# The first of 32 chunks of a recommendation kernel is loaded, multiplied and contracted in two halves, the second among layer 2's first banks, and ScalarE issues 11 of the first half's 23 loads

## What is computed

```python
e = jnp.stack([tbl_0[ids[:, 0]], ..., tbl_38[ids[:, 38]]], axis=1)      # (1024, 39, 16)
def _cin_layer(x0, xk, W, b):
    out = jnp.einsum('bhd,bmd,shm->bsd', xk, x0, W) + b[None, :, None]
    return jax.nn.relu(out)
x1 = _cin_layer(e, e, W1, b1)        # W1 (128, 39, 39)
x2 = _cin_layer(e, x1, W2, b2)       # W2 (128, 128, 39)
z = concatenate([x1.sum(-1), x2.sum(-1)], -1)
h = relu(concatenate([z, dense_ctx], 1) @ W_top1 + b_top1)
y = relu(h @ W_top2 + b_top2) @ W_top3
```

## Time and profile before

| | |
|---|---|
| median of 3 runs | 1172.12 us (1167.8 to 1173.06) |
| the profiled execution, its own time | 1171.53 us |
| its span, first to last instruction | 1169.7 us |
| PE busy, share of the span | 1089.3 us, 93% |
| DVE busy | 981.9 us, 84% |
| ACT busy | 822.2 us, 70% |
| POOL busy | 850.0 us, 73% |
| mean granted clock of TensorE | 0.999 |

### The profile page before, as it was taken

One profiled execution on the slowest core, in us unless ns is written; L12 is line 12 of the kernel. 1 busy time (PEld: TensorE's weight loads), 2 busy tenths in 40 slices (PEclk: granted clock), 3 DMA queues, 4 the chain that ended last, 5 costly groups with the idle time before them and its releaser, 6 DMA issues.

```text
span 1169.7 us, 18115 instructions
## 1 busy us (share of the span) xinstructions
PE 1089.3 (93%) x4475; PEld 824.1 (70%) x4475; DVE 981.9 (84%) x2893; ACT 822.2 (70%) x2774; POOL 850.0 (73%) x951
## 2 busy tenths in 40 slices
PE   0069999999999999999999999999999999999998
PEld 0037677677777777767777667777777777777687
DVE  4048999998988989998998668998899989996787
ACT  5027677777777777777777667777777777775774
POOL 7756888878787888788878758787887864543454
PEclk9999999999999999999999999999999999999999
DMA  6178678685877678684876538776787858665342
GB/s 182 29 161 182 123 145 179 147 168 106 188 163 147 135 154 180 145 168 100 195 162 150 110 70 189 167 145 130 154 185 154 168 110 201 146 147 104 73 85 52
DMA packets 82881, 166.61 MB, mean 142 GB/s; under 512 B 17812, under 2 KB 31014, under 8 KB 82775
## 3 DMA queue, kind: packets, MB, share of 16 engines
q0 software_dynamic: 28272, 85.81, 42.2%
q1 hardware_dynamic: 54502, 79.64, 24.3%
HBM read 78.36 MB, written 3.81 MB: 70 GB/s over the span
## 4 chain that ended last, share of the span: by engine, by line
PE 83%; DVE 9%; POOL 3%; issue 2%; SPq 1%; ACT 1%; DMA 1%; DVEq 0%; ACTq 0%
PE bank L821 66%; PE l_acc L806 14%; DVE acc L680 4%; POOL emb L404 3%; DVE t_sum L688 1%; PE misc L854 1%; PE misc L850 1%; DVE p2acc L698 1%; DVE x1l L645 0%; DVE p L721 0%; SPq L359 0%; DVE t_sum L692 0%; ACT prod L527 0%; DVE p1acc L655 0%; SPq L366 0%
## 5 line engine op out<-in xcount | busy, mean ns | idle before, releaser
L527 ACT ACTIVATE prod<-bank,emb 128x128 f32<-128x128 f32 x2552 | 715.8, 380 | 272.0 <-PE bank L821 269.5
L680 DVE SCALAR_TENSOR_TENSOR acc<-bank,emb,acc 128x128 f32<-128x128 f32 x2184 | 612.5, 345 | 68.1 <-PE bank L821 67.3
L821 PE MATMUL bank<-w2h,x1h 128*128 128x512 f32 (+1 forms) x1280 | 537.0, 420 | 10.4 <-DVE acc L680 8.2
L821 PE MATMUL bank<-w2l,x1h 128*128 128x512 f32 (+1 forms) x1280 | 494.4, 386 | 0.0
L821 PE MATMUL bank<-w2h,x1l 128*128 128x512 f32 (+1 forms) x1280 | 449.7, 417 | 0.0
L404 POOL DMA_INDIRECT emb<-tbl,idx x312 | 312.5, 1001 | 82.5 <-issue 77.9
L821 PEld LDWEIGHTS bank<-w2h,x1h 128*128 128x128 f32 x1280 | 241.0, 188 | 106.3 <-issue 44.7
L821 PEld LDWEIGHTS bank<-w2h,x1l 128*128 128x128 f32 x1280 | 240.6, 188 | 74.2 <-issue 20.3
L821 PEld LDWEIGHTS bank<-w2l,x1h 128*128 128x128 f32 x1280 | 241.0, 188 | 61.1 <-issue 22.1
L424 POOL TENSOR_TENSOR tree<-prod 128x640 f32<-128x640 f32 x127 | 237.2, 1868 | 55.0 <-DMA prod<-prod 55.0
L415 POOL DMA_DIRECT2D prod<-prod x127 | 123.6, 973 | 170.2 <-ACT prod L527 170.1
(11 more groups left out here) (105 smaller groups left out, 421.4 us busy)
## 6 DMA issues: line engine op xcount, KB each, us to landing
prod<-prod POOLq DMA_DIRECT2D x127, 640.0 KB
z<-e_rows SPq DMA_DIRECT2D x96, 234.0 KB
z<-e_rows SPq DMA_DIRECT2D x192, 78.0 KB
z<-e_rows SPq DMA_DIRECT2D x96, 156.0 KB
emb<-tbl,idx POOLq DMA_INDIRECT x312, 4.9
prod<-w_by_h SPq DMA_DIRECT2D x3, 832.0 KB, 8.4
z<-e_rows SPq DMA_DIRECT2D x32, 66.0 KB
e_rows<-e_t SPq DMA_DIRECT2D x8, 256.0 KB
```

Of the source, the lines that this page charges most:

```text
L527: last = nc.scalar.activation(prod[:, ct % P_RING, i, n * S:(n + 1) * S], bank[:, (ct * NB + k) % RING, n * S:(n + 1) * S], ACT.Copy, scal ...
L680: nc.vector.scalar_tensor_tensor(dst, src, scale, dst if step else b2_row[:, :], ALU.mult, ALU.add).then_inc(v_step, 1)
L821: last = nc.tensor.matmul(out_bank[:, 0:b - a], x, w[:, a:b], start=(n == 0), stop=(n == 2))
```

## The change

Chunk 0 is split into two halves of 256 columns. Half 0 runs ahead of the loop as the chunk did before. Half 1 is worked in among chunk 0's own banks: DVE makes its products at g = 1, 2, 3, PE contracts it at g = 7, 8, 9 and 11 into the PSUM tile `misc`, ACT ends it at g = 12, DVE forms `x1l` at g = 13; position 2 (g = 20) is the first that needs it. Half 1 multiplies from the SBUF rows without a copy to `e_rep`. Chunk 1's steps move: `copy_rep(1)` from ahead of bank 0 to between banks 0 and 2 on ACT, its seven products to g = 4, 6, 8, 11, 14, 16, 19 with `REST` fifth instead of third, its first contractions to g = 13, 15 and on. The loads of half 0 are shared: SP issues 12 (replicated rows, groups 1 and 2), ACT the other 11 (group 3, both factors of `REST`). SP issues all 23 of half 1 and then chunk 1's. Every transfer of a half moves the same number of rows as before, each of 1 KB instead of 2 KB.

```diff
+MAKE_SECOND_AT = (4, 6, 8, 11, 14, 16, 19)
+HALF = CH // 2
+HALF_MAKE_AT = {1: (0, 1, 2), 2: (3, 4), 3: (5, 6)}
+HALF_CONTRACT_AT = {7: (0, 1), 8: (2, 3), 9: (4, 5), 11: (6,)}
+HALF_ROUND_AT, HALF_MIX_AT = 5, 6
+HALF_X1_AT, HALF_X1L_AT, HALF_P1_AT = 12, 13, 14
...
-    if f == 0:
-        return tuple(range(NF))
+    if f == 1:
+        return (0, 1, 2, 3, REST, 4, 5)
...
+    if f == 1:
+        return {13: 0, 15: 1, 17: 2, 20: 3, 23: REST, 24: 4, 25: 5}
...
-                load_shifted(f)
                 if f == 0:
-                    load_rest_first(0)
+                    sp.wait_ge(et_stored[0], 64)
+                    load_half_rep(sp, 0)
+                    load_half_group(sp, 0, 0)
+                    load_half_group(sp, 0, 1)
+                    load_half_rep(sp, 1)
+                    for k in range(len(Z_GROUPS)):
+                        load_half_group(sp, 1, k)
+                    load_half_first(sp, 1)
+                    load_half_second(sp, 1)
+                else:
+                    load_shifted(f)
...
-            copy_rep(0)
-            for c in range(-1, CHUNKS):
+            act.wait_ge(et_stored[0], 64)
+            load_half_group(act, 0, 2)
+            load_half_first(act, 0)
+            copy_rep_half()
+            load_half_second(act, 0)
+            round_rest_half(0)
+            end_layer1_half(0)
+            for c in range(CHUNKS):
                 f = c + 1
                 for g in range(GB):
+                    if c == 0 and g == 1:
+                        copy_rep(1)
+                    if c == 0 and g == HALF_ROUND_AT:
+                        round_rest_half(1)
+                    if c == 0 and g == HALF_X1_AT:
+                        end_layer1_half(1)
...
+            def make_half(h, t):
+                rows = F_ROWS[t]
+                part = z[0:rows, 0, t, half(h)]
+                if t == REST:
+                    dve.wait_ge(half_first[h], 64)
+                    dve.wait_ge(half_second[h], 64)
+                    first = rest[0:rows, half(h)].bitcast(F32)
...
+                    first = z[0:rows, 0, NF, half(1)] if h else e_rep[0:rows, half(0)]
+                nc.vector.tensor_tensor(part, first, part, ALU.mult).then_inc(f_made if h else half_made, 1)
...
+                if c == 0 and j == 2 and k == 0:
+                    pe.wait_ge(x1l_done, 1)
```

More of the change, by code:

```diff
@@ L264, in gathers_before, with loads, half @@
             return min((TILES - 1) * M, -(-M * (ct + 9 + min(2, ct // 4)) // 16))
+        def loads(f):
+            return (f + 1) // 2
+        def half(h):
+            return slice(h * HALF, (h + 1) * HALF)
+        half_acc = (l1_acc[:, 0:HALF], misc[:, 0:HALF])
         def wait_early(eng, tile):
@@ L345, in load_shifted @@
                 wait(sp, f_used, NF * (f - 1))
-                wait(sp, rep_ready, f - 1)
+                wait(sp, rep_ready, f - 2)
                 def rows(first, ap):
@@ L510, in round_rest, with copy_rep_half, round_rest_half, end_layer1_half @@
                 nc.scalar.copy(rest[0:3 * N_REST, :], z[0:3 * N_REST, f % 2, REST, :]).then_inc(rest_high, 1)
+            def copy_rep_half():
+                act.wait_ge(half_rep[0], 64)
+                nc.scalar.copy(e_rep[:, half(0)], z[:, 0, NF, half(0)]).then_inc(half_copied, 1)
+            def round_rest_half(h):
+                part, parts = rest[0:3 * N_REST, half(h)], z[0:3 * N_REST, 0, REST, half(h)]
+                act.wait_ge(f_made if h else half_made, NF)
+                nc.scalar.copy(part, parts).then_inc(rest_high if h else half_high, 1)
+            def end_layer1_half(h):
+                act.wait_ge(f_used if h else half_used, NF)
+                nc.scalar.activation(half_acc[h], half_acc[h], ACT.Relu, bias=bias1[:, 0:1]
+                                     ).then_inc(x1_relu if h else half_relu, 1)
+                act.wait_ge(x1_relu if h else half_relu, 1)
+                nc.scalar.copy(x1h[:, 0, half(h)], half_acc[h]).then_inc(x1h_done if h else half_x1h, 1)
             def end_layer1(f):
@@ L747, in _ @@
                                         ).then_inc(top_split, 1)
-            for c in range(-1, CHUNKS):
+            for t in range(NF):
+                make_half(0, t)
+            mix_rest_half(0)
+            make_x1l_half(0)
+            sum_p1_half(0)
+            for c in range(CHUNKS):
                 f = c + 1
@@ L794, in contract @@
                 rows = F_ROWS[t]
-                if turn == 0:
-                    pe.wait_ge(w1_summed, 1)
-                    wait(pe, l1_free, f)
-                    wait(pe, x1l_done, f)
+                if turn == 0 and f == 1:
+                    pe.wait_ge(half_summed, 1)
+                    pe.wait_ge(half_x1l, 1)
+                if turn == 0 and f > 1:
+                    pe.wait_ge(l1_free, f)
+                    pe.wait_ge(x1l_done, f)
                 if t == REST:
@@ L806, in contract, with contract_half @@
                 nc.tensor.matmul(l1_acc[:, :], w, x, start=(turn == 0), stop=(turn == NF - 1)).then_inc(f_used, 1)
+            def contract_half(h, t):
+                rows = F_ROWS[t]
+                if t == 0:
+                    pe.wait_ge(w1_summed, 1)
+                if t == REST:
+                    pe.wait_ge(w_rest_mixed, 1)
+                    pe.wait_ge(rest_mixed if h else half_mixed, 1)
+                    w, x = w_rest[0:rows, :], rest[0:rows, half(h)]
+                else:
+                    pe.wait_ge(f_made if h else half_made, t + 1)
+                    w, x = w1[0:rows, t, :], z[0:rows, 0, t, half(h)]
+                nc.tensor.matmul(half_acc[h], w, x, start=(t == 0), stop=(t == REST)
+                                 ).then_inc(f_used if h else half_used, 1)
             def layer2_bank(c, j, k):
```

110 lines of the change are left out of this document (91 added, 19 removed).

## The result

The changed kernel takes 1177.76 us, the median of 11 runs (1173.45 to 1183.17); the kernel before, run beside it, takes 1168.66 (11 runs, 1164.4 to 1173.17). The ratio is 1.0068, 95% interval 1.0048 to 1.0088: slower by 5.6 to 10.3 us. The forecast was 2.4 us faster, 1169.7, with 1166 to 1174.5 as its range. It was wrong: the time moved the other way, by 9.1 us, and ended above the range, just under the 1178 beyond which the forecast had put 7 chances in 100. The profiled execution of the changed kernel took 1179.83 us, with a span of 1178.0.

A forecast was written before the change was run, and what follows sets the result against it. The prediction took PE, without slack from bank 0 on, as the bound, with loads and a chain of steps setting bank 0's start. Its terms, -6.6 + 2.7 + 1.5 = -2.4 us, gave 1169.7 us, range 1166 to 1174.5.

The forecast's parts named there:

- What bounds the kernel: PE is busy 99 to 100% from bank 0 on, so each us of earlier start or added wait counts at the end.
- Term 1: Before bank 0: half-width loads shared by SP and ACT start bank 0 at 71.4 instead of 77.96 us, -6.6 us.
- a packet of 1 KB lies between: Half 0's loads: 1 KB packets take 55 ns, so 1,078 of them move at 160 a us, in 6.7 us.
- is issued at 64.2: ACT's 11 loads of half 0: 7.3 us of issue and a 0.4 us copy, last one landing at 66.1.
- Term 2: Half 1's contractions on PE, formerly in idle time, now stand between chunk 0's banks: +2.7 us, called certain.
- Term 3: Chunk 0's banks: ACT waits for chunk 1's replicated rows, PE stalls before bank 7, +1.1 us; DVE's readout adds +0.4.
- due 3.4 us later than before: Chunk 1's last load meets product `REST` at g = 14 with five banks of slack behind it, at no cost.
- A PE wait among banks 15 to 20, released by DVE: Sign that the forecast is wrong: chunk 1's `REST` loads would come past 91.5 us.
- Small packets are no cheaper: Rival, 12 in 100: loads stay at 96 packets a us, bank 0 at 75.5, total 1175.2 us, or 1178.5 with backlog.
- ACT's issues are dear: Case inside the forecast: 1 us per ACT issue, bank 0 at 73.2, term 3's first part gone, -2.1 us in all.
- No wait at copy_rep(1): Rival, 18 in 100: chunk 1's replicated rows land by 76.5, term 3 is 0 to 0.2, total 1168.2 to 1166.4 us.
- Merges fall differently: Rival, 8 in 100: the 31 merges on DVE, at another phase to GpSimd, give or take 3 us or so.

The follow-up runs named there:

- e6: The changed kernel again, unchanged, beside the kernel before on another chip: 1177.09 us, ratio 1.0057 to the kernel before.
- e12: The kernel before, with GpSimd holding back tile 1's gathers until the first chunk's loads have landed: 1172.44 us in one run.
- e13: The changed kernel, with SP alone issuing all 23 loads of half 0: 1183.1 us, ratio 1.0101 to the kernel before.
- e11: The changed kernel, with SP issuing nothing of half 1 before all of half 0 has landed: 1180.37 us in one run.
- e9: The kernel before, with ScalarE issuing 11 of the first chunk's 23 loads, all in full width: 1171.59 us, ratio 1.0022.
- e8: The kernel before, with each of the first chunk's 23 loads cut into two pieces of 256 columns, all issued by SP: 1186.3 us, ratio 1.0121.
- e7: The changed kernel, with chunk 1's replicated rows issued before half 1's loads and an own tile for its first `REST` factor: 1178.93 us, ratio 1.0079 to the kernel before.

## Why the prediction was wrong

**What bounds the kernel** held up to chunk 1: PE has no slack from bank 0 on, and the start, the work and the waits add up to the 7.25 us lost at chunk 1's bank 0. That each of these us is a us of the end held only roughly: the spans lie 8.3 apart and the medians 9.1, but over lags that went down to 2.2 and up again, and in e6 a lag of 9.0 us at chunk 1 became 5.6 at the end. The forecast had no term for TensorE's clock behind a stall in the banks, and left merges at nothing in its sum.

**Term 1, an earlier bank 0: -6.6 forecast, -1.9 measured (-0.1 in the repeat).** The step that failed is "a packet of 1 KB lies between ... I take 55. Half 0 has 1,078 of them, so at 96 x 92 / 55 = 160 a us". The rate was 107 a us while it mattered. I had turned the time that a packet fills an engine into a rate, though the earlier trace rows showed the engines 55% busy with these packets and 80% with the gathers: the packets' own time wasn't the limit (e12: 58% busy, 100 a us), and making them shorter did not lift it. The count had a second fault. 1.29 MB are only 630 packets of 2 KB, so nearly a fifth of the 769 were much smaller ones and not rows: rows went at 79 a us before and, with 0.70 MB of 1 KB each, at 85 after. The 512 B packets of the earlier trace rows were 852 in 2 us, many more in a us, but they were stores from 128 partitions (`e_rows<-e_t`, one issue of 0.39 us for 256 KB), another kind of transfer. The second half of that step, ACT's part "is issued at 64.2", took until 66.63. Half 0's rows came at nearly the full chunk's pace in rows, not in bytes (e13, e11), and the second issuer brought about a tenth (e9). The Trainium skill (DMA: Bandwidth & Descriptors, Rules for kernel authors) says that issuing from several engines brings no bandwidth. By that rule ScalarE's share could not lift the rate, and e9's 104 packets a us for 96 nearly agree. The same section of the Trainium skill says that transfers below 64 KB pay mostly overhead. For the issue e8 agrees: 12.4 us for the narrow ones, 14.6 for the full. The forecast gave both only the weight of a rival, on the ground of the earlier trace rows. Behind the landing the six products took 2.07 us for 2.25, but from product `REST` to bank 0 it was 4.42 instead of 3.3, since PE's contractions of the five others, 3.99 us from 70.48 on, were still running.

**Term 2, half 1 on PE: +2.7 forecast, +3.6 measured as PE's extra busy time.** Right in kind. The 0.9 beyond it is resolved in part only. The clock is in it with both signs and about cancels: 1.00 instead of 0.59 from 78 to 82 us, then 0.51 from 87.3 to 90.8, behind the 4.46 us stall. Some 0.3 is how idle time is counted: two bank matmuls start 0.23 us apart but each lasts 0.39, so each of the two stalls costs 0.16 more than its idle time (an estimate).

**Term 3, ACT's wait: +1.1 forecast, +4.46 measured; DVE: +0.4 and +1.10.** The mechanism was right, with its buffer and its bank (before bank 7); its two inputs were off. Chunk 1's rows landed at 84.73 instead of 78.1: SP was held up by 1.1 + 1.3 + 1.8 + 1.6 us in the four places shown above, where 1.0 in all was allowed, and the rows took 5.3 us to land instead of 3.5. And PE came to bank 7 at 81.99 instead of 78.7. Of the 6.6 us by which the rows were late, 3.3 were hidden because bank 0 was late too. For the last load of chunk 1, "due 3.4 us later than before ... at no cost", the step left out SP's own wait: `load_rest_first(1)` needs `f_used`, which half 1 now raises at g = 11. The loads went out at 92.92 (76.27 in the kernel before), the product came at 101.55 (88.89 before). It was in the code, and the rule to go through every queue that a moved step stands ahead of would have found it. "A PE wait among banks 15 to 20, released by DVE" was the forecast's own sign for this, and it is there.

**The rivals.** "Small packets are no cheaper" was what happened, with 12 chances in 100: it said bank 0 at 75.5 (76.1), replicated rows at 83.7 (84.7), 2.6 us lost before bank 7 (4.46), 1175.2 to 1178.5 us (1177.76). It had the rate nearly right. That its sum of +3.1 us, or 6.4 with the backlog, comes so near the measured 9.1 is partly luck, since merges and the clock moved the end by as much. What made me weigh it low was the one row with small packets, whose transfers are not of this kind. "It turns to a loss where the rows land after 80.5, each us beyond costs one" held too: 84.73 - 80.5 = 4.2 us, beside 4.46 measured. "ACT's issues are dear" did not happen as it was meant (1.36 and 3.17 us for three and four; the last four took 4.14, held up like SP's), nor did "No wait at copy_rep(1)". "Merges fall differently" is real and of the size it gave, 3 us a step, of either sign: the lag went from 7.25 down to 2.2 and back to 5.2.

**The sum.** Forecast -6.6 + 2.7 + 1.5 = -2.4; measured -1.87 + 3.56 + 5.56 = +7.25. Of the 9.7 between them 4.7 stand in term 1 and 3.4 in the first part of term 3, both from the rate of packets; 0.9 in term 2, and 0.7 in the second part of term 3, to which the rate and SP's overlooked wait both add. The rest of the way to the medians, where +9.1 stands against -2.4, is merges and clock; how the two share it no run tells.

## What to carry to other kernels

Before you cost a transfer by its size, look at what the queue moved and how busy all queues together kept the engines: where these had room, the time of a packet isn't the rate, halving the bytes halved nothing here, and transfers issued and packets moved were the better price. Splitting a tile in two doubles both for everything behind it, so ask first which load stands last in the queue and who reads it; a second issuer changes the order more than the rate, so give it only what is needed last. And where a step moves behind others, list each wait of each queue on its counter, the loading engine's too. Last, when two kernels are compared to a per cent, compare their granted clocks over all runs before you give the difference a cause.

## What the runs showed of the hardware

- From 58 to 66 us, loads of rows to 11 to 39 partitions moved at 96 to 107 packets a us with 2 KB and with 1 KB packets, from one queue or from two (96 before, 107 after, 104 in e9, 100 in e13 and in e12). Over 58 to 80 us it was 91 before, 98 in e13 and in e8, 106 after; the highest stretch was 147 (66 to 72 us, after).
- The price of an issue goes with the shape and not with the row's length: 0.40 us for 39 rows of one to three tiles, 0.76 for the `REST` loads of 21 to 30 rows, at 256 columns as at 512. Loads behind a backlog wait: three narrow ones took 2.29 and 2.97 us with two issuers where they took 1.20 with SP alone (e13), but three full ones took 3.00 with SP alone too.
- One chip of those used took 1183.6 us for the kernel before instead of 1169, with issues of 0.70 us in this stretch and a mean clock of 0.993 instead of 0.998 to 0.999; the edit that hands loads to ScalarE changes sign there (0.995 for 1.002), with a mean clock of 0.998 in its own runs.
- TensorE's clock: after the 4.46 us stall it stood at 0.51 from 87.3 to 90.8 us, so at the lower of its two levels, though the engine was busy all of that time; after the 4.33 us stall of e6 it was 0.50 from 85.6 to 92.2 us. In e7, where no wait among the banks was longer than 1.73 us, it was 1.00 from 77 to 118 us.
